# A recurrent time-mix on one core: score products on 32x32 tiles, added up in PSUM

## Chip, core and metric

The kernel runs on one core of one Trainium2 chip. The metric is the device time of one execution in microseconds. The time of the kernel before is the median of three runs.

## The reference, cut to what matters

Two parts are computed from the same normed rows and added to the input: a recurrent time-mix (16 heads of 32 channels, 2 sequences of 4096 tokens) and a layer of eight experts. The change is in the time-mix. Its recurrence is

```python
def step(S, inp):
    r_, w_, k_, v_, kk_, b_ = inp
    sab = jnp.einsum('bhvk,bhk->bhv', S, kk_)
    S = S * jnp.exp(w_)[:, :, None, :] + sab[..., None] * b_[:, :, None, :] + v_[..., None] * k_[:, :, None, :]
    y = jnp.einsum('bhvk,bhk->bhv', S, r_)
    return (S, y)
_, y = jax.lax.scan(step, S0, (rh, wh, kh, vh, kkh, bh))
```

The kernel doesn't step through tokens. It takes 32 tokens at a time as a chunk and, for each head, forms the products of queries (`kk` for the u part, `r` for the y part) with keys (`b` and `k`) of the same chunk, with the decay between them. Only earlier keys count: key < query for u, key <= query for y. The products are the entries of small triangular systems, which are inverted by doubling.

## The kernel before

**Tiles and stages.** The time-mix goes in 64 tiles of 128 columns, 64 tokens of each of the two sequences. Channels are on the partitions: 4 groups (G) of 128 channels, each with 4 heads (HG) of 32. A *unit* is one group, one sequence and one chunk of 32 tokens; a tile has U = 16 units. The work is a pipeline of five stages: N (norm the rows), A (projections), B (scores), C (inverse and state), D (output). One *turn* runs all five, each on another tile (`step`). 68 turns are laid out, most of them inside a loop whose body has 28 turns written out; scores are made in 64.

**Order.** Nothing schedules the work: each engine has its order written by hand (`DVE_STEPS`, `ACT_STEPS`, `POOL_STEPS`, `PE_STEPS`), and the functions `on_vector`, `on_scalar`, `on_gpsimd` and `on_tensor` issue it. Each step raises the engine's semaphore by one; others wait for the count. PSUM has eight banks, and `BANK` lists their tenants in order: `clear(e, name)` makes TensorE wait until the tenant before has been read.

**The scores (stage B).** Decay within a chunk is split in four *blocks* of eight queries (BLOCKS = 4): block j takes its reference at its own middle and needs keys 0 to 8j+7, so 8, 16, 24 and 32 keys, KEYS = 80 in all. VectorE makes the keys for the four blocks (`key_span`, `make_keys`) in `keys`: for each unit 2 x 80 columns (b and k). GpSimd makes the queries (`queries_of`, L774): for each of the four heads a product over 32 partitions, written into the head's own 32 columns of a 128-column slab, the rest of which is zero from a fill at the start. So a slab has the four heads' queries on its block diagonal, and TensorE (`score`, L877) needs one product for a unit: 128x128 weights, 160 columns moving. In the result each partition has a head's query and the columns are all four blocks' keys. For three units at a time (two in the last groups, `UNITS`) VectorE takes out what counts (`mask_scores`, L378): four predicated copies, one for each block, with a mask `known` of the queries of that block and the keys before them, into `raw`, which was filled with zero at the start. That is 6 groups x 4 blocks x 2 (u, y) = 48 predicated copies a turn. Their tenants in PSUM are u0 to u5 and y0 to y5, in banks 4 and 5 in turn, with `bonus` before u0 in bank 4, `out` in bank 4 and `gate` in bank 5.

**What stands around.** On TensorE the score groups stand between the products of the inverse (`P_of` L853, `Q_of` L864: 64 products on 32x32 tiles each, in two halves), the projections (`project` L829, 128x128), the low-rank ones (`low` L838), the output (`out_of` L947) and the state (`from_values` L891, `from_state` L905, `u_of` L915, `from_solved` L924: 32 products on 32x32 tiles each). In the 32x32 products head h uses partitions 32h to 32h+31 for its operands and its result. VectorE has `B.bonus` (L477), `D.acc` (L551, adds the stored rows to the output), the predicated copies of the inverse (`invert`, L403) and 32x32 transposes.

A float32 product shows as two matmul records in the trace, each with its own weight load.

Of the kernel before, what the change touches and what calls it, by code (L numbers as in the profile page):

```python
# [8 lines left out]
P = 128  # L9
# [80 lines left out]
UNITS = [(0, 3), (3, 6), (6, 9), (9, 12), (12, 14), (14, 16)]  # L90
# [26 lines left out]
def time_mix(nc, core, dram):  # L117
# [3 lines left out]
    with ExitStack() as ctx:  # L121
# [11 lines left out]
        for name, width in (("known", 4 * KEYS), ("levels", 5 * N)):  # L133
            wt[name] = sb(name, width, I32)
# [73 lines left out]
        known = wt["known"][:, :].rearrange("p (q o s k) -> p q o s k", q=2, o=1, s=2)  # L208
# [6 lines left out]
        heads_of = lambda q: queries[q][:, :].rearrange("p (n h j s) -> p n h j s", n=U, h=HG, j=BLOCKS)  # L215
# [25 lines left out]
        for g in range(G):  # L241
# [14 lines left out]
            "B.y5.3 A.scan A.b A.k2 C.rows1 C.shrunk1 C.state1").split()  # L256
# [5 lines left out]
            "B.rk B.eye B.qu0 B.qu1 B.qu2 B.qu3 B.qy0 B.qy1 B.qy2 B.qy3 C.faded0 A.lt B.us C.faded1 B.ys").split()  # L262
        PE_STEPS = (
            "A.x D.centre C.P0 A.mix A.scored C.Q0 D.var A.delta D.gate B.value C.P1 B.bonus A.gate1 A.low_wa A.delta3 B.u0 C.Q1 "
            "B.u1 A.low_k C.P2 B.u2 C.Q2 A.key B.u3 A.decay C.P3 B.u4 B.u5 A.low2 C.Q3 B.y0 B.y1 A.sums C.z0 B.y2 "
            "B.y3 C.u0 C.y0 D.out B.y5 B.y4 C.z1 C.u1 A.recept C.y1").split()
# [6 lines left out]
            ("centre", 4, dve, "D.normed"), ("bonus", 4, dve, "B.bonus"), ("u0", 4, dve, "B.u0.3"), ("u2", 4, dve, "B.u2.3"),  # L273
            ("u4", 4, dve, "B.u4.3"), ("y0", 4, dve, "B.y0.3"), ("y2", 4, dve, "B.y2.3"), ("out", 4, dve, "D.acc"),
            ("y4", 4, dve, "B.y4.3"), ("var", 5, act, "D.lnv"), ("gate", 5, dve, "D.gated"), ("u1", 5, dve, "B.u1.3"),
            ("u3", 5, dve, "B.u3.3"), ("u5", 5, dve, "B.u5.3"), ("y1", 5, dve, "B.y1.3"), ("y3", 5, dve, "B.y3.3"),
            ("y5", 5, dve, "B.y5.3"), ("P0", 6, act, "C.P0"), ("P1", 6, act, "C.P1"), ("P2", 6, act, "C.P2"),
# [63 lines left out]
        def on_vector(e, turn, on, out, got):  # L341
# [4 lines left out]
            def query_span():  # L346
                if "B.shrink" in act.was:
                    e.wait_ge(act.old, act.ago("B.shrink"))
                    e.wait_ge(pool.old, pool.ago(f"B.qy{HG - 1}"))
                e.tensor_tensor(by_block(dq), refs, spans, ALU.subtract).then_inc(dve.sem, dve.step("B.dq"))  # L350

            def key_span(j):
                if j == 3 and "B.y5" in pe.was:
                    e.wait_ge(pe.old, pe.ago("B.y5"))
# [12 lines left out]
            def mask_scores(q, m):  # L367
# [124 lines left out]
            if Bs:  # L492
                mask_scores("u", 0)
                mask_scores("u", 1)
            if A:
                lerp_of(3)
            if Bs:
                mask_scores("u", 2)
            if Cs:
                invert(2)  # L500
            if Bs:
                mask_scores("u", 3)
# [11 lines left out]
            if Bs:  # L514
                mask_scores("u", 4)
                mask_scores("u", 5)
                e.wait_ge(dve.sem, dve["B.u5.3"])
# [12 lines left out]
            if Bs:  # L530
                mask_scores("y", 0)
                mask_scores("y", 1)
# [5 lines left out]
            if Bs:  # L538
                mask_scores("y", 2)
# [7 lines left out]
                mask_scores("y", 3)  # L547
# [12 lines left out]
            if Bs:  # L560
                mask_scores("y", 4)
# [14 lines left out]
            if Bs:  # L576
                mask_scores("y", 5)
# [184 lines left out]
        def on_gpsimd(e, turn, on, out, got):  # L762
# [58 lines left out]
        def on_tensor(e, turn, on, out, got):  # L821
# [201 lines left out]
            if Bs:  # L1023
                score("u", 0)
# [687 lines left out]
```

## Time and profile before

| | |
|---|---|
| median of three runs | 6587.33 us (6576.18 to 6587.72) |
| the profiled execution, span | 6580.5 us |
| instructions in the profile | 269852 |
| TensorE matmul, busy | 5958.9 us (91%), 123464 |
| TensorE weight load, busy | 4298.1 us (65%) |
| VectorE, busy | 4111.1 us (62%), 9325 |
| ScalarE, busy | 1874.8 us (28%) |
| GpSimd, busy | 1465.7 us (22%), 1284 |
| mean granted TensorE clock | 0.955 |

How to read the profile: PE is TensorE's matmul side, PEld its weight loads, DVE VectorE, ACT ScalarE, POOL GpSimd, SP SyncE. Times are microseconds from the start of the span. A group of instructions is told by its line, engine and operation, with the tiles that it writes and reads, its shape and its count. An idle time has behind "<-" what ended it; "issue" means that nothing the profile shows did. The ends of matmuls are modelled and overlap the next start, so in a timeline the distance between starts is the safer measure.

### The profile page before, as it was taken

What the parts mean: (1) busy time and instruction counts of PE and PEld (TensorE: products, weight loads), DVE (VectorE), ACT (ScalarE), POOL (GpSimd) and SP (SyncE); (2) the same over time, 40 slices, a digit from 0 to 9 for tenths busy, and PEclk for the clock granted to TensorE, in tenths of its full rate; (3) what the DMA queues carried; (4) which work ended last, traced back from release to release, by engine and by line L of the source; (5) the groups of instructions that cost most, each with busy time, mean ns of one, the idle gap of its engine ahead of it and who ended that gap; (6) DMA issues with size and microseconds to landing.
All of it is one profiled execution on the core that took longest, in us unless ns stands there. A gap on an engine that the chain in (4) does not pass through costs nothing. (4 is left out here: it accounts for less than half of the span.)

```text
span 6580.5 us, 269852 instructions
## 1 busy us (share of the span) xinstructions
PE 5958.9 (91%) x123464; PEld 4298.1 (65%) x123464; DVE 4111.1 (62%) x9325; ACT 1874.8 (28%) x3531; POOL 1465.7 (22%) x1284
## 2 busy tenths in 40 slices
PE   6898898999998898998989898897499999999999
PEld 5777777777777777777777777776244444444443
DVE  6778787778777778777778778776424223322300
ACT  3333333333333333333333333332010000000010
POOL 1222222222222222222222222221202202221210
PEclk9999999999999999999999999998699999999999
DMA  1000000000000000000000000000211211121120
GB/s 56 20 18 17 20 19 16 18 21 16 20 20 16 19 21 16 18 21 16 18 21 16 17 23 16 17 21 10 92 45 57 81 58 66 59 91 45 66 71 13
DMA packets 108741, 212.80 MB, mean 32 GB/s; under 512 B 25424, under 2 KB 26704, under 8 KB 107088
## 3 DMA queue, kind: packets, MB, share of 16 engines
q1 hardware_dynamic: 92240, 144.98, 7.6%
q0 software_dynamic: 15360, 50.48, 2.3%
q8 instruction: 977, 16.01, 1.0%
q14 instruction: 164, 1.34, 0.1%
HBM read 144.67 MB, written 50.72 MB: 30 GB/s over the span
## 5 line engine op out<-in xcount | busy, mean ns | idle before, releaser
L378 DVE COPY_PREDICATED time_raw<-time_known,w_bank 128x96 f32<-128x96 int32 (+6 forms) x3072 | 823.4, 274 | 209.3 <-PE w_bank L877 127.9
L1664 PE MATMUL moe_bank<-moe_w,moe_hidden 128*128 128x512 f32 x2048 | 928.7, 596 | 0.0
L1651 PE MATMUL moe_bank<-moe_hT,moe_w 128*128 128x512 f32 x2048 | 923.3, 594 | 0.8 <-DVE moe_hT L1551 0.8
L1651 PEld LDWEIGHTS moe_bank<-moe_hT,moe_w 128*128 128x128 f32 x2048 | 386.4, 190 | 471.3 <-issue 470.1
L1664 PEld LDWEIGHTS moe_bank<-moe_w,moe_hidden 128*128 128x128 f32 x2048 | 379.4, 190 | 429.5 <-issue 428.1
L1572 ACT ACTIVATE moe_hidden<-moe_bank,moe_b 128x512 f32<-128x512 f32 x256 | 175.9, 687 | 1628.2 <-PE moe_bank L1651 1491.5
L806 POOL TENSOR_TENSOR time_tail<-time_tail,time_lp 128x512 f32<-128x512 f32 x64 | 75.4, 1178 | 2288.7 <-ACT time_lp L733 2222.2
L877 PE MATMUL w_bank<-time_keys,time_queries_u 128*128 128x160 f32 x2048 | 424.4, 353 | 146.9 <-DVE time_bonus L477 141.9
L864 PE MATMUL w_bank<-time_invT,time_part 32*32 32x32 f32 x32768 | 426.1, 201 | 123.7 <-issue 67.6
L864 PEld LDWEIGHTS w_bank<-time_invT,time_part 32*32 32x32 f32 x32768 | 363.3, 112 | 209.4 <-issue 143.3
L853 PEld LDWEIGHTS w_bank<-time_inv,time_ub 32*32 32x32 f32 x32768 | 348.0, 109 | 166.7 <-issue 129.4
L877 PEld LDWEIGHTS w_bank<-time_keys,time_queries_u 128*128 128x128 f32 x2048 | 347.5, 223 | 161.5 <-DVE time_bonus L477 148.7
L853 PE MATMUL w_bank<-time_inv,time_ub 32*32 32x32 f32 x32768 | 410.0, 198 | 45.5 <-issue 30.3
L774 POOL TENSOR_TENSOR time_queries_u<-time_dq,time_kkn 32x512 f32<-32x512 f32 x256 | 312.6, 1221 | 475.3 <-ACT time_dq L648 460.3
L403 DVE COPY_PREDICATED time_invT<-time_levels,w_bank 128x512 f32<-128x512 int32 x256 | 187.2, 731 | 362.4 <-PE w_bank L864 362.3
L1551 DVE COPY moe_hT<-moe_bank 128x512 f32<-128x512 f32 x64 | 44.2, 691 | 536.2 <-PE moe_bank L1638 536.2
L877 PE MATMUL w_bank<-time_keys,time_queries_y 128*128 128x160 f32 x2048 | 343.3, 310 | 27.5 <-DVE time_mixed L551 19.9
L774 POOL TENSOR_TENSOR time_queries_y<-time_dq,time_r 32x512 f32<-32x512 f32 x256 | 353.1, 1379 | 25.9 <-POOL time_queries_u L774 10.0
L877 PEld LDWEIGHTS w_bank<-time_keys,time_queries_y 128*128 128x128 f32 x2048 | 292.3, 191 | 82.8 <-DVE time_mixed L551 34.9
L393 DVE SCALAR_TENSOR_TENSOR time_lerp<-w_bank,time_maa,time_xx 128x128 f32<-128x128 f32 x1024 | 284.5, 340 | 55.5 <-PE w_bank L932 55.4
L829 PE MATMUL w_bank<-time_xf,time_value 128*128 128x128 f32 x2048 | 291.1, 293 | 0.1
L829 PE MATMUL w_bank<-time_xf,time_key_w 128*128 128x128 f32 x2048 | 283.1, 287 | 0.0
(227 smaller groups left out, 10059.2 us busy)
## 6 DMA issues: line engine op xcount, KB each, us to landing
moe_w<-in_w SPq DMA_DIRECT2D x64, 1024.0 KB, 7.4
mid_xn<-time_xn_rows SPq DMA_DIRECT2D x128, 129.0 KB, 2.5
time_x_rows<-in_x SPq DMA_DIRECT2D x128, 128.0 KB, 2.9
time_base<-in_x SPq DMA_DIRECT2D x128, 128.0 KB, 3.2
mid_acc<-time_mixed SPq DMA_DIRECT2D x128, 128.0 KB, 2.7
mid_scores<-time_rated SPq DMA_DIRECT2D x128, 2.0 KB
moe_b<-in_b SPq DMA_DIRECT2D x8, 256.0 KB
time_receptance<-in_w_receptance SPq DMA_DIRECT2D x1, 1024.0 KB, 5.0
```

The costliest lines, as they stand in the source:

```text
L378: e.copy_predicated(by_raw[:, "uy".index(q), n0:n1, :, 0:8 * j + 8], known[:, "uy".index(q), :, :, mine].to_broadcast([P, n1 - n0, 2, 8 * ...
L393: e.scalar_tensor_tensor(grp(lerp, g), grp(BANK[f"delta{f}"], g), wt["maa"][:, f * G + g:f * G + g + 1], grp(xx, g), ALU.add, ALU.mult).th ...
L403: e.copy_predicated(chunks(got["invT"]), level(lev + 1, U), chunks(BANK[f"Q{lev}"])).then_inc(dve.sem, dve.step(f"C.T{lev}"))
L774: e.tensor_tensor(heads_of(q)[head(h), :, h], by_block(dq)[head(h), :, :, at:at + 8], eights(by)[head(h)], ALU.mult).then_inc(pool.sem, po ...
L806: e.tensor_tensor(chunks(tail), chunks(tail), padded(lp)[:, :, 1:33], ALU.add).then_inc(pool.sem, pool.step("A.lt"))
L829: mm = e.matmul(ps[:, o * P:(o + 1) * P], weight[:, g * width + o * P:g * width + (o + 1) * P], rhs_of(g), start=g == 0 and (o == 0 or not ...
L853: mm = e.matmul(BANK[f"P{lev}"][head(h), blk(n)], got["ub"][head(h), blk(n)], got["inv"][head(h), blk(n)], start=True, stop=True, skip_gro ...
L864: mm = e.matmul(BANK[f"Q{lev}"][head(h), blk(n)], part[head(h), blk(n)], got["invT"][head(h), blk(n)], start=True, stop=True, skip_group_c ...
L877: mm = e.matmul(BANK[f"{q}{m}"][:, (n - n0) * 2 * KEYS:(n - n0 + 1) * 2 * KEYS], queries[q][:, n * P:(n + 1) * P], keys[:, n * 2 * KEYS:(n ...
L1572: e.activation(hidden[now % 4][:, :], up[now % 3][:, :], ACT.Gelu_apprx_tanh, bias=b1[:, x * FC + k:x * FC + k + 1]).then_inc(act.sem, act ...
L1651: got = e.matmul(up[now % 3][:, :], w1[:, g * F + k * P:g * F + (k + 1) * P], hT[x % 2][:, g * CAP + half * HALF:g * CAP + (half + 1) * HA ...
L1664: got = e.matmul(down[t][:, :], hidden[now % 4][:, t * P:(t + 1) * P], tile(w2, k), start=k == 0, stop=k == FC - 1)
```

## The change

Scores are made for each head and block by itself. A query slab now has four blocks of 32 columns, one for each block of eight queries; block j has its eight queries in columns 8j to 8j+7 and zero elsewhere, for all four heads at once (each head on its own 32 partitions). GpSimd writes a slab in one instruction for u and one for y. TensorE takes, for each unit, blocks 3, 2, 1, 0 and in each the four heads: a product on a 32x32 tile with 2 x (8j+8) columns moving, added in PSUM to what is there; block 3 starts the sum and writes all 32 keys. As the other queries' columns are zero, each query's row ends with its own block's score. In PSUM a unit then has 2 x 32 columns, and eight units fill a bank. VectorE needs one predicated copy of 128x512 for eight units, with one causal mask that no longer knows blocks. The orders of steps and the tenants of banks follow: u0, y0 in bank 4, u1, y1 in bank 5, and TensorE issues the scores in six places, of four or eight units.

```diff
-UNITS = [(0, 3), (3, 6), (6, 9), (9, 12), (12, 14), (14, 16)]
+UNITS = [(0, 8), (8, 16)]
...
-        for name, width in (("known", 4 * KEYS), ("levels", 5 * N)):
+        for name, width in (("known", 2 * N), ("levels", 5 * N)):
...
-        heads_of = lambda q: queries[q][:, :].rearrange("p (n h j s) -> p n h j s", n=U, h=HG, j=BLOCKS)
+        eights_of = lambda q: bass.AP(tensor=queries[q], offset=0, ap=[[U * P, P], [P, U], [N + 8, BLOCKS], [1, 8]])
...
         PE_STEPS = (
-            "A.x D.centre C.P0 A.mix A.scored C.Q0 D.var A.delta D.gate B.value C.P1 B.bonus A.gate1 A.low_wa A.delta3 B.u0 C.Q1 "
-            "B.u1 A.low_k C.P2 B.u2 C.Q2 A.key B.u3 A.decay C.P3 B.u4 B.u5 A.low2 C.Q3 B.y0 B.y1 A.sums C.z0 B.y2 "
-            "B.y3 C.u0 C.y0 D.out B.y5 B.y4 C.z1 C.u1 A.recept C.y1").split()
+            "A.x D.centre C.P0 A.mix A.scored C.Q0 D.var A.delta D.gate B.value C.P1 B.bonus A.gate1 A.low_wa A.delta3 C.Q1 "
+            "B.u0 A.low_k C.P2 C.Q2 A.key A.decay C.P3 B.u1 A.low2 C.Q3 A.sums C.z0 B.y0 "
+            "C.u0 C.y0 D.out B.y1 C.z1 C.u1 A.recept C.y1").split()
...
                 e.wait_ge(pe.sem, pe[f"B.{q}{m}"])
-                got_ = BANK[f"{q}{m}"][:, 0:(n1 - n0) * 2 * KEYS].rearrange("p (n s k) -> p n s k", s=2, k=KEYS)
-                for j in range(BLOCKS):
-                    if j:
-                        e.wait_ge(dve.sem, dve[f"B.{q}{m}.{j - 1}"])
-                    mine = slice(key_at(j), key_at(j + 1))
-                    e.copy_predicated(
-                        by_raw[:, "uy".index(q), n0:n1, :, 0:8 * j + 8],
-                        known[:, "uy".index(q), :, :, mine].to_broadcast([P, n1 - n0, 2, 8 * j + 8]),
-                        got_[:, :, :, mine]).then_inc(dve.sem, dve.step(f"B.{q}{m}.{j}"))
+                e.copy_predicated(
+                    by_raw[:, "uy".index(q), n0:n1],
+                    known[:, "uy".index(q)].to_broadcast([P, n1 - n0, 2, N]),
+                    BANK[f"{q}{m}"][:, :].rearrange("p (n s t) -> p n s t", s=2, t=N)).then_inc(
+                    dve.sem, dve.step(f"B.{q}{m}"))
...
             def queries_of(q, at, by):
-                for h in range(HG):
-                    e.wait_ge(pool.sem, pool[f"B.q{q}{h}"] - 1)
-                    e.tensor_tensor(heads_of(q)[head(h), :, h], by_block(dq)[head(h), :, :, at:at + 8],
-                                    eights(by)[head(h)], ALU.mult).then_inc(pool.sem, pool.step(f"B.q{q}{h}"))
-                e.wait_ge(pool.sem, pool[f"B.q{q}{HG - 1}"])
+                e.tensor_tensor(eights_of(q), by_block(dq)[:, :, :, at:at + 8], eights(by), ALU.mult).then_inc(
+                    pool.sem, pool.step(f"B.q{q}"))
...
-            def score(q, *which):
-
-                for m in which:
+            def score(q, m, part_=(0, 8)):
+
+                if part_[0] == 0:
                     clear(e, f"{q}{m}")
                     e.wait_ge(dve.sem, dve["B.kk0"])
-                    e.wait_ge(pool.sem, pool[f"B.q{q}{HG - 1}"])
-                    n0, n1 = UNITS[m]
-                    for n in range(n0, n1):
-                        mm = e.matmul(BANK[f"{q}{m}"][:, (n - n0) * 2 * KEYS:(n - n0 + 1) * 2 * KEYS],
-                                      queries[q][:, n * P:(n + 1) * P], keys[:, n * 2 * KEYS:(n + 1) * 2 * KEYS],
-                                      start=True, stop=True, skip_group_check=True)
+                    e.wait_ge(pool.sem, pool[f"B.q{q}"])
+                n0, n1 = UNITS[m]
+                into = BANK[f"{q}{m}"][:, :].rearrange("p (n s t) -> p n s t", s=2, t=N)
+                for i in range(*part_):
+                    for j in reversed(range(BLOCKS)):
+                        for h in range(HG):
+                            mm = e.matmul(into[head(h), i, :, 0:8 * j + 8],
+                                          queries[q][head(h), (n0 + i) * P + j * N:(n0 + i) * P + (j + 1) * N],
+                                          by_key[head(h), n0 + i, :, key_at(j):key_at(j + 1)],
+                                          start=j == BLOCKS - 1, stop=j == 0, skip_group_check=True)
+                if part_[1] == n1 - n0:
                     mm.then_inc(pe.sem, pe.step(f"B.{q}{m}"))
...
-    mask = np.stack([(query // 8 == block) & m for m in (key < query, key <= query) for _ in "bk"], 1)
+    mask = np.stack([i < t, i <= t], 1)
```

In TensorE's order the scores move so: u0 (all eight units) stands behind both halves of the second Q (`Q_of(1, 1)`); the first half of u1 before `P_of(3, 0)`, its second half before `Q_of(3, 0)`; the first half of y0 before `from_values(0)`, its second half before `u_of(0)`; y1 before `from_values(1)`. On VectorE the mask of u0 follows `C.uk`, that of u1 follows `C.yk`, that of y0 follows `C.z0`, that of y1 follows `A.fk`.

## Rows read from the trace of the kernel before

**Rows 1.** The page: busy time, share of the span and instructions of each engine.

```profile
PE 5958.9 (91%) x123464; PEld 4298.1 (65%) x123464; DVE 4111.1 (62%) x9325; ACT 1874.8 (28%) x3531; POOL 1465.7 (22%) x1284
```

**Rows 2.** Windows: stretch, length, busy time (count) by engine, clock, DMA share, GB/s.

```profile
2028.60:2098.47 69.87, 63.95 (x1850) 53.76 (x1850) 55.30 (x131) 26.29 (x51) 17.22 (x15) 0.95 0.08 19
4400.00:4600.00 200.00, 164.25 (x5391) 134.65 (x5395) 131.12 (x307) 59.34 (x108) 37.17 (x34) 0.91 0.05 13
4600.00:4800.00 200.00, 103.56 (x1021) 58.71 (x1010) 90.67 (x179) 14.98 (x23) 39.02 (x33) 0.66 0.23 76
```

**Rows 3.** TensorE's waits: waiter, releaser, us in total, times, longest.

```profile
PE w_bank L877 <- DVE time_bonus L477: 141.9, 61, 3.9
PE w_bank L864 <- issue: 67.6, 60, 1.8
...
PE w_bank L877 <- DVE time_mixed L551: 19.9, 62, 0.7
```

**Rows 4.** The page's groups: busy us, mean ns of one, idle before.

```profile
L378 DVE COPY_PREDICATED time_raw<-time_known,w_bank 128x96 f32<-128x96 int32 (+6 forms) x3072 | 823.4, 274 | 209.3 <-PE w_bank L877 127.9
...
L806 POOL TENSOR_TENSOR time_tail<-time_tail,time_lp 128x512 f32<-128x512 f32 x64 | 75.4, 1178 | 2288.7 <-ACT time_lp L733 2222.2
...
L774 POOL TENSOR_TENSOR time_queries_u<-time_dq,time_kkn 32x512 f32<-32x512 f32 x256 | 312.6, 1221 | 475.3 <-ACT time_dq L648 460.3
L403 DVE COPY_PREDICATED time_invT<-time_levels,w_bank 128x512 f32<-128x512 int32 x256 | 187.2, 731 | 362.4 <-PE w_bank L864 362.3
...
L774 POOL TENSOR_TENSOR time_queries_y<-time_dq,time_r 32x512 f32<-32x512 f32 x256 | 353.1, 1379 | 25.9 <-POOL time_queries_u L774 10.0
```

**Rows 5.** Timeline of TensorE in a turn: start, us, group, count.

```profile
2080.87 1.90 PE L877 MATMUL w_bank<-time_keys,time_queries_y 128*128 128x160 f32 x12
2082.70 0.75 PE L915 MATMUL w_bank<-time_rhs,time_invT 32*32 32x32 f32 x64
2083.38 1.98 PE L947 MATMUL w_bank<-time_output,time_mixed 128*128 128x512 f32 x4
...
2091.43 1.16 PE L829 MATMUL w_bank<-time_xf,time_receptance 128*128 128x128 f32 x8
2092.52 1.10 PE L905 MATMUL w_bank<-time_by_state,time_state 32*32 32x64 f32 x64
2093.54 2.05 PE L829 MATMUL w_bank<-time_xf,time_receptance 128*128 128x128 f32 x16
2095.52 0.75 PE L915 MATMUL w_bank<-time_rhs,time_invT 32*32 32x32 f32 x64
```

**Rows 6.** The page's DMA queues: packets, MB, share of 16 engines.

```profile
q8 instruction: 977, 16.01, 1.0%
```

**Rows 7.** Timeline of TensorE near 4540 us; idle time before in brackets.

```profile
4539.95 1.08 PE L864 MATMUL w_bank<-time_invT,time_part 32*32 32x32 f32 x104 [0.66 <-issue]
4540.96 1.08 PE L877 MATMUL w_bank<-time_keys,time_queries_u 128*128 128x160 f32 x6
4542.70 0.33 PE L853 MATMUL w_bank<-time_inv,time_ub 32*32 32x32 f32 x17 [0.66 <-DVE time_raw L378]
4543.67 1.14 PE L853 MATMUL w_bank<-time_inv,time_ub 32*32 32x32 f32 x111 [0.65 <-issue]
4544.74 1.35 PE L877 MATMUL w_bank<-time_keys,time_queries_u 128*128 128x160 f32 x8
4546.02 0.26 PE L864 MATMUL w_bank<-time_invT,time_part 32*32 32x32 f32 x8
4547.52 1.22 PE L864 MATMUL w_bank<-time_invT,time_part 32*32 32x32 f32 x120 [1.23 <-issue]
4548.67 1.22 PE L877 MATMUL w_bank<-time_keys,time_queries_y 128*128 128x160 f32 x7
4551.47 0.95 PE L877 MATMUL w_bank<-time_keys,time_queries_y 128*128 128x160 f32 x5 [1.59 <-issue]
...
4555.59 0.31 PE L905 MATMUL w_bank<-time_by_state,time_state 32*32 32x64 f32 x7 [0.90 <-issue]
```

More of the change, by code:

```diff
@@ L250, in time_mix @@
             "B.kb1 B.kk1 B.kb0 B.kk0 B.bonus D.bonus D.gated C.T1 C.I1 "
[5 rows of a table removed]
-            "B.y5.3 A.scan A.b A.k2 C.rows1 C.shrunk1 C.state1").split()
[2 rows of a table added]
+            "B.ub C.T3 B.pairs B.inv "
+            "A.min C.z0 B.y0 B.vT B.kT B.bT "
+            "D.acc C.rows0 C.shrunk0 C.state0 A.kkn C.z1 A.wmk A.g1 A.p2 A.fk B.y1 "
+            "A.scan A.b A.k2 C.rows1 C.shrunk1 C.state1").split()
         ACT_STEPS = (
@@ L272, in time_mix @@
             ("rated", 3, dve, "A.rated"), ("delta0", 3, dve, "A.lerp03"), ("gate1", 3, act, "A.hid_g"), ("key", 3, dve, "A.kkn"),
[L273 to L277, printed above, removed]
+            ("centre", 4, dve, "D.normed"), ("bonus", 4, dve, "B.bonus"), ("u0", 4, dve, "B.u0"), ("y0", 4, dve, "B.y0"), ("out", 4, dve, "D.acc"),
+            ("var", 5, act, "D.lnv"), ("gate", 5, dve, "D.gated"), ("u1", 5, dve, "B.u1"),
+            ("y1", 5, dve, "B.y1"), ("P0", 6, act, "C.P0"), ("P1", 6, act, "C.P1"), ("P2", 6, act, "C.P2"),
             ("P3", 6, act, "C.P3"), ("sums0", 6, act, "C.y0"), ("sums1", 6, act, "C.y1"), ("Q0", 7, dve, "C.T0"), ("Q1", 7, dve, "C.T1"),
@@ L348, in query_span @@
                     e.wait_ge(act.old, act.ago("B.shrink"))
-                    e.wait_ge(pool.old, pool.ago(f"B.qy{HG - 1}"))
+                    e.wait_ge(pool.old, pool.ago("B.qy"))
                 e.tensor_tensor(by_block(dq), refs, spans, ALU.subtract).then_inc(dve.sem, dve.step("B.dq"))
             def key_span(j):
-                if j == 3 and "B.y5" in pe.was:
-                    e.wait_ge(pe.old, pe.ago("B.y5"))
+                if j == 3 and "B.y1" in pe.was:
+                    e.wait_ge(pe.old, pe.ago("B.y1"))
                 e.tensor_tensor(key_units(1, j), padded(csum)[:, :, 1:8 * j + 9],
@@ L514, in on_vector @@
             if Bs:
-                mask_scores("u", 4)
-                mask_scores("u", 5)
-                e.wait_ge(dve.sem, dve["B.u5.3"])
+                mask_scores("u", 1)
+                e.wait_ge(dve.sem, dve["B.u1"])
                 if c_was:
@@ L790, in on_gpsimd @@
                 e.wait_ge(dve.old, dve.ago("A.kkn"))
-                if "B.y5" in pe.was:
-                    e.wait_ge(pe.old, pe.ago("B.y5"))
+                if "B.y1" in pe.was:
+                    e.wait_ge(pe.old, pe.ago("B.y1"))
                 queries_of("u", 0, kkn)
@@ L795, in on_gpsimd @@
                 e.wait_ge(act.old, act.ago("A.r"))
-                if "B.y5" in pe.was:
-                    e.wait_ge(pe.old, pe.ago("B.y5"))
+                if "B.y1" in pe.was:
+                    e.wait_ge(pe.old, pe.ago("B.y1"))
                 queries_of("y", 1, r)
@@ L1027, in on_tensor @@
             if Bs:
-                score("u", 1)
+                score("u", 0, (0, 4))
+                score("u", 0, (4, 8))
             if Cs:
@@ L1037, in on_tensor @@
                 key_of(0, 2)
-            if Bs:
-                score("u", 2)
             if Cs:
@@ L1048, in on_tensor @@
             if Bs:
-                score("u", 3)
+                score("u", 1, (0, 4))
             if Cs:
@@ L1061, in on_tensor @@
             if Bs:
-                score("u", 4)
-                score("u", 5)
+                score("u", 1, (4, 8))
             if Cs:
@@ L1077, in on_tensor @@
             if Bs:
-                score("y", 0)
-                score("y", 1)
+                score("y", 0, (0, 4))
             if Cs:
@@ L1089, in on_tensor @@
             if Bs:
-                score("y", 2)
-                score("y", 3)
+                score("y", 0, (4, 8))
             if Cs:
@@ L1102, in on_tensor @@
             if Bs:
-                score("y", 5)
-                score("y", 4)
+                score("y", 1)
             if Cs:
@@ L1179, in time_mix_inputs @@
     one = lambda name: d[name].reshape(1, C)
-    query, block = np.arange(P)[:, None] % N, np.repeat(np.arange(4), 8 * np.arange(1, 5))[None]
-    key = np.concatenate([np.arange(8 * j + 8) for j in range(4)])[None]
-    mask = np.stack([(query // 8 == block) & m for m in (key < query, key <= query) for _ in "bk"], 1)
+    mask = np.stack([i < t, i <= t], 1)
     heads = row // N == np.arange(P)[None] // N
```

21 lines of the change are left out of this document (4 added, 17 removed), and 7 rows, old and new, of the table DVE_STEPS.

## Prediction

> **How I read it.** The page comes first: TensorE's matmuls fill 91% of the span and VectorE 62% [rows 1]. That share is a mean over two stages, so the stretches come next. The change sits in the first of them, the time-mix; the expert matmuls behind it don't change. One turn of the time-mix, from one set of transposes of the normed rows to the next, takes 69.87 us (2028.60 to 2098.47), with 1850 matmul records, 63.95 us of them busy, at a mean granted clock of 0.95 [rows 2]. So in a turn TensorE has six idle microseconds and everybody else many more: it is the engine that sets the turn. There are 64 turns with scores (3072 masks at 48 a turn [rows 4]).
>
> The waits say what the six microseconds are: 141.9 us in all, 2.2 a turn, are the first score product waiting for VectorE's bonus (its bank is the bonus's), 19.9 us (0.3 a turn) are the product of y4 waiting for `D.acc`, and 67.6 us of one tiled line alone are put down to "issue", that is, to nothing that the profile shows [rows 3]. This last kind decides the case, so I followed it in the timeline.
>
> **What "issue" is.** Near 4540 us the turns run with less beside the tiled work, and the stall returns again and again: matmuls start anew, after an idle time that nothing releases, at 4539.95, 4543.67, 4547.52 and 4551.47 [rows 7]. Twice it cuts a group of tiled products in the middle, where no wait stands in the code. Count the records between: 104+6+17 = 127, then 111+8+8 = 127, then 120+7 = 127. Each matmul record has a weight load beside it, so 127 are 254 instructions, and a couple of semaphore waits make 256. The page lists a DMA queue of kind "instruction" with 977 packets and 16.01 MB [rows 6], 16.4 KB each; 2 x 123,464 TensorE instructions [rows 1] over 977 are 253 to a packet. So TensorE's program comes in pieces of 256 instructions, and where a piece is used up before the next is there, TensorE stands still. The spacings of those starts, 3.72, 3.85 and 3.95 us (mean 3.84), are what a piece costs when it is run through quicker than that. Only the first of the three has a wait for VectorE in it, and it is the shortest, so such waits don't make the spacing. I take the mean, and 3.72 for the low end. Today a turn has 2 x 1850 instructions, about 14.5 pieces in 69.9 us, or 4.8 us each: mostly slower than the fetch, so it shows in few places.
>
> The Trainium skill, in "Runtime: NRT & Kernel Launch", section "Instruction fetch mechanics", gives the same piece (16 KiB, 256 instructions) and says that the crossing is mostly hidden, since the sequencer fetches the next one meanwhile. The rows agree on the piece and not on the hiding: that rule would take the sum below to that of the first rival.
>
> **Part by part, for one turn.**
>
> *TensorE, removed:* 32 products of 128x128 weights with 160 columns, two records each, 64 records. Twelve of them take 1.83 us from their start to the next line's (2080.87 to 2082.70), 0.152 us each [rows 5]: 9.8 us.
>
> *TensorE, added:* 16 units x 4 blocks x 4 heads x 2 (u and y) = 512 products on 32x32 tiles; each is again two records, as in the 32x32 lines of today: 1024 records of 64, 48, 32 and 16 columns, a quarter each. Price by the array: 64 records of 32 columns take 0.68 us (2082.70 to 2083.38) [rows 5], 104 take 1.01 us (4539.95 to 4540.96) [rows 7]; the 40 more cost 0.33 us, so 8.25 ns each and 0.15 us for the change of shape. 64 records of 64 columns take 1.02 us (2092.52 to 2093.54) [rows 5], 13.6 ns each. For 16 columns I have no row; they are no dearer than 32 and, since the pitch is then no longer that of the columns, probably no cheaper: 8.25. 48 lies between: 11. The mean is 10.3 ns, 10.5 us a turn (8.4 if all went at 8.25). Accumulating instead of overwriting costs nothing in the 64-column row, which accumulates too.
>
> *Changes of shape:* eight full records take 1.09 us, sixteen 1.98 [rows 5], so 0.111 each and 0.20 fixed; with the tile's 0.15 a round trip between the shapes costs 0.35. The scores now stand next to tiled groups, and five full stretches disappear (between Q1 halves, before P2, before Q3, before `from_values(0)`, before `u_of(0)`): -1.7 us. By the array alone TensorE's turn gets 1.0 us shorter.
>
> *TensorE's program:* 960 more records, 1920 more instructions: 2 x 2810 = 5620 a turn, 22 pieces where it was 14.5. The added 2048 are 8 pieces, and each is run through in 128 x 10.3 ns = 1.3 us, so it costs the fetch's 3.84: 30.7 us. This is the step on which the sum hangs.
>
> *VectorE:* 48 masks a turn (823.4 us in all, 12.9 a turn) become four of 128x512 from PSUM; the predicated copy of that shape takes 731 ns [rows 4]: 2.9. Ten microseconds less, none on TensorE's path except through the bonus wait. That wait (2.2 us) goes: VectorE reaches `B.bonus` earlier, as GpSimd is beside it for a shorter time, and TensorE later; where it goes nothing else is late, for the fetch is then what ends last. The 0.3 us on `D.acc` goes as y1 is in bank 5.
>
> *GpSimd:* 8 products of 32x512 (1221 and 1379 ns, 10.4 us a turn) become two of 128x512, 1178 ns each by the nearest row [rows 4]; strided, up to 1.4. Eight microseconds less, hidden both before and after behind TensorE. Fewer semaphore steps: nothing.
>
> *Added waits:* u and y have two banks, not six tenancies. `out_of` needs the mask of y0, which starts when y0's last product is through and takes 0.73 us; `u_of(0)`'s 0.68 us stands between, so TensorE waits 0.1 to 0.3 us: +0.2. Behind it are only TensorE's own products. y1 in front of `from_values(1)` holds up the state by its length, which is already in the sum. Mask u1 has both halves of Q3 and the low-rank products to hide under. The smaller mask constant shortens one load at the start: nothing.
>
> *Clock:* the mean granted clock is 0.95 where TensorE is 92% busy (2028.60), 0.91 at 82% (4400), 0.66 at 52% (4600) [rows 2]. The new turn has some 62 us of work in 90, 70%: between the last two, 0.8. What would be slowed is the other work, some 50 us: at most 50 x (0.95/0.8 - 1) = 9 us. Most of that falls into pieces that wait for the fetch anyway or where the clock is up again, so I take 3, with 0 and 9 as ends.
>
> **The sum.** The rest of a turn: 69.9 - 9.8 (scores) - 2.2 - 0.3 (waits) - 1.7 (shape) + 0.2 = 56.1 us. With 30.7 for the eight pieces and 3 for the clock: 89.8 us, 19.9 more than 69.9. Times 64: +1274 us. Against the profiled execution (span 6580.5, 7 us under the median of the runs shown, which is 6587.3) this is 7855, against the median 7861. I predict 7860.
>
> Two errors in it work against each other: score groups don't begin at a piece's edge, so a piece that is half score and half slower work pays less than I count; and tiled P and Q groups next to them, now hidden half the time, fall under the fetch more often. Lower end: all 22 pieces of a turn at the shortest spacing, 3.72: 81.8 us, +11.9 x 64 = 762, 7350. Upper end: eight pieces at 4.12 us (the next spacing in rows 7, 4551.47 to 4555.59) and the clock's 9 us: 56.1 + 33.0 + 9 = 98.1, +28.2 x 64 = 1805, 8390. I round this to 8380.
>
> **Rivals.**
> 1. *The fetch is hidden* (faster). If a piece could be had as fast as it is run through, or several lay ready ahead, a turn would be 56.1 + 10.5 = 66.6 us, with the clock as now: -3.3 x 64 = -211, 6376. For it: most pieces cross without a stall today. Against: the four starts in a row at equal numbers of instructions, with 3.7 to 3.95 us between; had three or more pieces lain ready, the second and third stall could not be. The point at which it decides: the change loses time as soon as a dense piece costs over (69.9 - 56.1)/8 = 1.7 us. Chance 0.07. This is where the skill's "mostly hidden" would lead.
> 2. *The fetch comes later and the clock falls for good* (slower still). After a stall the next piece may come later (the one behind 4551.47 takes 4.12 us, again with nothing released in it), and a half clock after each of the six score groups slows what follows. 98 us a turn or above, 8390. For it: 0.66 at 52% busy. Against: the clock in a turn comes back quickly today. Chance 0.15, half of it above my range.
> 3. *The tiles don't overlap in accumulation* and go one after another: 4 x 10.3 = 41 ns a record, 42 us a turn in place of 30.7: 56.1 + 42 + 3 = 101, 8590. Against: the 64-column row. Chance 0.03.
> 4. *Pieces shared well*: pieces that are part score and part slow work balance each other, and a piece that is run through in 1.3 us, quicker than any in rows 7, has its successor asked for sooner than 3.72: a turn of 75 to 81 us, 6900 to 7350. For it: no row is as dense. Against it: nothing in the spacings falls with the work in them. Chance 0.08.
>
> The forecast has 0.66, and 0.01 is left for an end between rivals 1 and 4. So faster by over 0.2% (13 us, about what a measurement of this kernel can tell from no change) 0.07, within it 0.01, slower 0.92. The range leaves out rivals 1, 3 and 4 and half of rival 2, near 2 in 10 with a little over; I don't stretch it to 6900, since rival 4 has no row of its own behind it.
>
> **What would show it.** 184,904 TensorE matmuls; the instruction queue at some 24 MB; "issue" as TensorE's longest wait, over 1000 us in all, standing in the score line and at equal distances of 127 or 128 records, with 3.7 to 4 us between; TensorE's busy share in a turn near 70%; a turn of 85 to 95 us; VectorE's masks at 256 of about 0.73 us; no wait of the scores for the bonus. Right about the array: a score group without a stall in it has 10 ns a record. I'm wrong if 256-instruction pieces in the score line follow at under 3 us, or if the longest wait there is one for VectorE or GpSimd.

## The result, and the profile after

| | before | after |
|---|---|---|
| median | 6587.5 us (6576.2 to 6597.2, 4 runs) | 7863.7 us (7845.7 to 7876.1, 4 runs) |
| ratio to before | | 1.1936, 95% interval 1.1915 to 1.1957 |
| profiled execution, span | 6580.5 us | 7843.9 us |
| mean granted TensorE clock | 0.955 | 0.879 |

The change makes the kernel 19% slower, 1276 us, or 19.9 us for each of the 64 turns with scores. 7860 was forecast.

The page of after, busy time by engine, the clock in 40 slices, and the instruction queue (packets, MB, share of 16 engines):

```profile
PE 6531.3 (83%) x184904; PEld 4828.6 (62%) x184904; DVE 3280.0 (42%) x6509; ACT 1878.4 (24%) x3531; POOL 938.2 (12%) x900
...
PEclk8888888888888888888888888888877999999999
...
q8 instruction: 1456, 23.86, 1.3%
```

Against [rows 1] and [rows 6]: VectorE has 831 us less to do and GpSimd 528; both only stand idle longer. TensorE has 61,440 matmul records more, 960 in each of 64 turns, and its program is 7.85 MB longer.

One turn of after in the windows view, with the columns of [rows 2]:

```profile
2013.70:2104.50 90.80, 72.59 (x2817) 62.32 (x2818) 43.35 (x88) 26.32 (x51) 9.03 (x9) 0.85 0.06 16
```

The turn went from 69.87 to 90.80 us. Of the 20.9 us more, 8.6 are work (72.59 against 63.95, some of it the same work at the lower clock) and 12.3 are idle time.

TensorE's waits in after (waiter, releaser, us in total, times, longest); L859 is the score line, L832, L843, L875 and L899 are lines of tiled products that the change doesn't touch:

```profile
PE w_bank L859 <- issue: 597.1, 380, 3.0
PE w_bank L832 <- issue: 163.3, 115, 2.5
PE w_bank L843 <- issue: 94.6, 82, 2.4
PE w_bank L875 <- issue: 91.8, 65, 3.0
PE w_bank L899 <- issue: 65.9, 32, 2.7
...
PE w_bank L931 <- DVE time_raw L371: 9.3, 30, 0.3
```

These five are 1012.7 us, where [rows 3] began with 141.9 us of waiting for the bonus and 67.6 of issue. Over all lines of this view, issue is 1052.8 us, and 115.3 in the kernel before. So of the 1263 us by which the two profiled executions differ, 937 are more issue. The waits for other engines have become shorter together, and none of the five longest has a releaser. The last row is the wait that the change adds, the output product for the mask of y0, 0.15 us a turn.

What such a wait looks like, in the timeline of TensorE in that turn (start, us, group, count, idle before):

```profile
2035.36 0.84 PE L859 MATMUL w_bank<-time_keys,time_queries_u 32*32 32x64 f32 x64
2038.40 1.83 PE L859 MATMUL w_bank<-time_keys,time_queries_u 32*32 32x64 f32 x128 [2.19 <-issue]
2042.42 1.37 PE L859 MATMUL w_bank<-time_keys,time_queries_u 32*32 32x64 f32 x64 [2.19 <-issue]
2043.61 1.05 PE L832 MATMUL w_bank<-time_inv,time_ub 32*32 32x32 f32 x63
2046.29 0.21 PE L832 MATMUL w_bank<-time_inv,time_ub 32*32 32x32 f32 x1 [1.63 <-issue]
...
2055.02 1.50 PE L859 MATMUL w_bank<-time_keys,time_queries_u 32*32 32x64 f32 x128
2056.34 0.38 PE L832 MATMUL w_bank<-time_inv,time_ub 32*32 32x32 f32 x21
```

Count the records from one stall to the next: 128, then 64+63 = 127. That is [rows 7] again, now in the middle of the scores, with 4.02 and 3.87 us between. The group at 2055.02 has no stall inside: its 128 records take 1.32 us to the next group's start, 10.3 ns each. So a piece of the program that the array runs through in 1.3 us costs the turn close to four.

The counts say that the stalls keep step with the program; that it is the arrival of the program which ends them, the DMA view shows. From 2034 to 2044 us, in 40 slices of 0.25 us, nothing moves but three packets of the instruction queue, 16 KB each:

```profile
DMA  0000003000000000000000300000000000000030
GB/s 0 0 0 0 0 0 66 0 0 0 0 0 0 0 0 0 0 0 0 0 0 0 66 0 0 0 0 0 0 0 0 0 0 0 0 0 0 0 66 0
```

They start in the slices at 2035.5, 2039.5 and 2043.5 us, and TensorE goes on at 2038.40, 2042.42 and 2046.29, 2.8 to 2.9 us behind the slice's start each time. The whole trace has the same order. It holds 723 idle times of TensorE that are put down to issue; 98% of them end 1.2 to 1.6 us after a packet of this queue has ended. For matmul records picked at even distances that holds in 10% of cases. In the kernel before it is 95% of 137, against 7%. The medians in after make up the distance between stalls: from TensorE's new start to the next packet 1.2 us, the packet 1.1 us, from its end to TensorE's next start 1.4 us, 3.7 together. None of the three is work on the array.

VectorE's masks and GpSimd's queries in after (busy us, mean ns of one, idle before):

```profile
L371 DVE COPY_PREDICATED time_raw<-time_known,w_bank 128x512 f32<-128x512 int32 x256 | 185.4, 724 | 821.5 <-PE w_bank L859 821.5
L754 POOL TENSOR_TENSOR time_queries_y<-time_dq,time_r 128x512 f32<-128x512 f32 x64 | 76.9, 1201 | 0.0
```

### The profile page after: what moved, and what is told of

Read it like the earlier page. It is cut to its first block and busy times, and to the rows that moved or that the text cites. A ratio compares the mean times of both kernels' runs of the same rounds, so it can differ in the third digit from the quotient of the medians.

```text
span 7843.9 us, 388891 instructions
## 1 busy us (share of the span) xinstructions
PE 6531.3 (83%) x184904; PEld 4828.6 (62%) x184904; DVE 3280.0 (42%) x6509; ACT 1878.4 (24%) x3531; POOL 938.2 (12%) x900
## 3 DMA queue, kind: packets, MB, share of 16 engines
q8 instruction: 1456, 23.86, 1.3%
## 5 line engine op out<-in xcount | busy, mean ns | idle before, releaser
L859 PE MATMUL w_bank<-time_keys,time_queries_u 32*32 32x64 f32 (+3 forms) x32768 | 506.8, 216 | 343.7 <-issue 342.2
L859 PEld LDWEIGHTS w_bank<-time_keys,time_queries_u 32*32 32x32 f32 x32768 | 461.5, 122 | 381.4 <-issue 372.9
L859 PE MATMUL w_bank<-time_keys,time_queries_y 32*32 32x64 f32 (+3 forms) x32768 | 463.4, 207 | 257.0 <-issue 254.8
L859 PEld LDWEIGHTS w_bank<-time_keys,time_queries_y 32*32 32x32 f32 x32768 | 427.0, 114 | 328.6 <-issue 327.2
L832 PE MATMUL w_bank<-time_inv,time_ub 32*32 32x32 f32 x32768 | 467.5, 207 | 168.8 <-issue 163.3
L832 PEld LDWEIGHTS w_bank<-time_inv,time_ub 32*32 32x32 f32 x32768 | 397.2, 119 | 275.6 <-issue 245.5
L843 PE MATMUL w_bank<-time_invT,time_part 32*32 32x32 f32 x32768 | 440.5, 205 | 131.5 <-issue 94.6
L371 DVE COPY_PREDICATED time_raw<-time_known,w_bank 128x512 f32<-128x512 int32 x256 | 185.4, 724 | 821.5 <-PE w_bank L859 821.5
L843 PEld LDWEIGHTS w_bank<-time_invT,time_part 32*32 32x32 f32 x32768 | 380.4, 116 | 193.3 <-issue 157.6
L412 DVE STREAM_TRANSPOSE time_rhs<-w_bank 128x256 f32<-128x256 f32 x128 | 57.6, 450 | 934.8 <-PE w_bank L889 934.8
L875 PE MATMUL w_bank<-time_by_values,time_vT 32*32 32x96 f32 x8192 | 308.6, 309 | 94.8 <-issue 91.8
L875 PEld LDWEIGHTS w_bank<-time_by_values,time_vT 32*32 32x32 f32 x8192 | 259.7, 139 | 112.4 <-issue 109.4
L808 PE MATMUL w_bank<-time_xf,time_receptance 128*128 128x128 f32 x2048 | 308.9, 304 | 2.6 <-issue 2.6
```

What stands on the lines that cost most here:

```text
L371: e.copy_predicated(by_raw[:, "uy".index(q), n0:n1], known[:, "uy".index(q)].to_broadcast([P, n1 - n0, 2, N]), BANK[f"{q}{m}"][:, :].rearr ...
L412: e.transpose(chunks(rhs), sums[:, :, at["z"] // N]).then_inc(dve.sem, dve.step(f"C.z{c}"))
L808: mm = e.matmul(ps[:, o * P:(o + 1) * P], weight[:, g * width + o * P:g * width + (o + 1) * P], rhs_of(g), start=g == 0 and (o == 0 or not ...
L832: mm = e.matmul(BANK[f"P{lev}"][head(h), blk(n)], got["ub"][head(h), blk(n)], got["inv"][head(h), blk(n)], start=True, stop=True, skip_gro ...
L843: mm = e.matmul(BANK[f"Q{lev}"][head(h), blk(n)], part[head(h), blk(n)], got["invT"][head(h), blk(n)], start=True, stop=True, skip_group_c ...
L859: mm = e.matmul(into[head(h), i, :, 0:8 * j + 8], queries[q][head(h), (n0 + i) * P + j * N:(n0 + i) * P + (j + 1) * N], by_key[head(h), n0 ...
```

## The experiments

**The disputed cost by itself.** 2048 tiled records in a row ahead of the first turn of the kernel before:

```diff
         core.meet((core.consts_in, CONSTS))
+        for n in range(16 * 16):
+            for h in range(HG):
+                nc.tensor.matmul(psum[7][head(h), blk(n % 16)], wt["ident"][head(h), 0:N], wt["eye"][head(h), :],
+                                 start=True, stop=True, skip_group_check=True)
```

> The kernel before with 1024 products on 32x32 tiles of 32 columns (2048 records, 16 pieces) back to back ahead of the first turn, nothing beside them. Theory of the pieces: 16 x 3.6 us = 55 to 60 us longer, with a stall each 128 records. Rival (array): 2048 x 8.3 ns = 17 us longer, without stalls.

Measured: 6632.7 us in one execution, 44 us over the median of before on that chip (7 runs, 6578.8 to 6596.3). The products themselves take 58.7 us (28.00 to 86.67), within the 55 to 60. The first turn's transposes start at 86.67 us, where they start at 31.8 in before, so 3.8 us of the products fill time in which TensorE waited anyway; the other 11 us between 55 and 44 aren't explained, and a single execution can't settle them. Its timeline, TensorE:

```profile
28.00 2.99 PE L1139 MATMUL w_bank<-time_eye,time_ident 32*32 32x32 f32 x212 [1.03 <-PEq L80]
32.32 1.58 PE L1139 MATMUL w_bank<-time_eye,time_ident 32*32 32x32 f32 x128 [1.33 <-issue]
36.32 1.93 PE L1139 MATMUL w_bank<-time_eye,time_ident 32*32 32x32 f32 x128 [2.42 <-issue]
...
50.96 1.93 PE L1139 MATMUL w_bank<-time_eye,time_ident 32*32 32x32 f32 x128 [1.52 <-issue]
54.69 1.93 PE L1139 MATMUL w_bank<-time_eye,time_ident 32*32 32x32 f32 x128 [1.79 <-issue]
58.69 1.93 PE L1139 MATMUL w_bank<-time_eye,time_ident 32*32 32x32 f32 x128 [2.07 <-issue]
...
85.89 0.85 PE L1139 MATMUL w_bank<-time_eye,time_ident 32*32 32x32 f32 x44 [1.80 <-issue]
86.67 1.11 PE L956 MATMUL w_bank<-time_ident,time_xn_rows 128*128 128x128 f32 x4
```

No other engine works on these operands, no semaphore stands between the products, and TensorE still stops each 128 records, for 1.33 to 2.42 us. From 32.32 to 85.89 there are fourteen pieces: 53.57 us, 3.83 us each, at 3.45 to 4.01. Only at the start does more than one piece seem to lie ready (212 = 84 + 128 records without a stall). This is the price that the forecast had taken from three spacings, 3.84. The granted clock is 0.52 in this stretch, near the lower level of 1.2 GHz, and a piece takes the array 1.93 us there. At that pace all 2048 records would be 31 us, so the low clock doesn't make the 58.7 either; and the pieces of [rows 7] came at the same distance while the tiled groups ran at full pace.

**The same number of products with more and with less work in each.** In the first all four blocks are replaced by block 3, and each product overwrites instead of adding; in the second every block has only its first eight keys, and the mask leaves out the rest:

```diff
-                    for j in reversed(range(BLOCKS)):
+                    for j in (3, 3, 3, 3):
...
-                                          start=j == BLOCKS - 1, stop=j == 0, skip_group_check=True)
+                                          start=True, stop=True, skip_group_check=True)
```

```diff
-                            mm = e.matmul(into[head(h), i, :, 0:8 * j + 8],
+                            mm = e.matmul(into[head(h), i, :, 0:8],
                                           queries[q][head(h), (n0 + i) * P + j * N:(n0 + i) * P + (j + 1) * N],
-                                          by_key[head(h), n0 + i, :, key_at(j):key_at(j + 1)],
+                                          by_key[head(h), n0 + i, :, key_at(j):key_at(j) + 8],
...
-    mask = np.stack([i < t, i <= t], 1)
+    mask = np.stack([(i < t) & (i < 8), (i <= t) & (i < 8)], 1)
```

> The change with the same count of products, but block 3's query columns and keys in all four places (the other blocks' scores are left out): every record has 64 columns instead of 16, 32, 48 and 64. Theory of the pieces: the array has room under the fetch (128 x 13.6 ns = 1.7 us of 3.6), so the time stays within 1% of 7864. Rival (array): (13.6 - 10.3) ns x 1024 x 64 = 216 us more, 8080.

> The change with the same count of products, but only the first eight keys for every block (the later keys are left out and masked): every record has 16 columns. Theory of the pieces: the same as after, 7800 to 7880, with 16 and 64 columns within 1.5% of each other. Rival (array): 1024 x 2.1 x 64 = 134 us less, 7730, and 350 us between 16 and 64 columns.

Measured: with 64 columns 7739.6 us (ratio to before 1.1759, 1.1732 to 1.1786), with 16 columns 7926.3 (1.2044, 1.2015 to 1.2072). Four times the work on the array is 187 us *faster*. That refutes the array as the bound, which wanted 350 us the other way. It is not what the pieces alone say either: they wanted 7785 to 7943 and 7800 to 7880, with the two within 1.5% of each other; the first is below, the second above, and the distance is 2.4%. The windows from 1000 to 4000 us of the kernels with 64 columns, of after, and with 16 columns, columns as in [rows 2]:

```profile
1000.00:4000.00 3000.00, 2415.43 (x94463) 2055.40 (x94462) 1438.07 (x2907) 885.27 (x1717) 304.32 (x305) 0.94 0.07 16
```

```profile
1000.00:4000.00 3000.00, 2401.97 (x92732) 2040.02 (x92731) 1406.29 (x2840) 870.40 (x1684) 297.60 (x297) 0.86 0.06 16
```

```profile
1000.00:4000.00 3000.00, 2411.45 (x91510) 2033.63 (x91505) 1392.19 (x2812) 862.56 (x1668) 297.53 (x297) 0.80 0.06 16
```

The granted clock is 0.94, 0.86 and 0.80 in this order. What it does to the products that the change doesn't touch can be read from the groups view: added up over all of the time-mix but the scores, their busy time is 3772, 4047 and 4229 us, and 3613 in before. The pieces don't differ: where a piece holds nothing but scores, it takes 3.53, 3.57 and 3.56 us. So the added work is free under the fetch, and with it the clock stays up for the slower products beside the scores. The clock is a second cost of its own in after, some 7863.7 - 7739.6 = 124 us, 1.9 us a turn. Probably it is more, for with 64 columns the untouched products still take 159 us longer than in before. (The two medians are from different chips; by the ratios to before it is 117. The kernel with 64 columns also overwrites where after adds up, which isn't tested apart.)

**Fewer products.** Only block 3, and only blocks 3 and 1:

```diff
-                    for j in reversed(range(BLOCKS)):
+                    for j in (BLOCKS - 1,):
...
-                                          start=j == BLOCKS - 1, stop=j == 0, skip_group_check=True)
+                                          start=True, stop=True, skip_group_check=True)
```

```diff
-                    for j in reversed(range(BLOCKS)):
+                    for j in (3, 1):
...
-                                          start=j == BLOCKS - 1, stop=j == 0, skip_group_check=True)
+                                          start=j == 3, stop=j == 1, skip_group_check=True)
```

> The change with only block 3 of the four scored for each unit and head (blocks 0 to 2 left out of the sum): 256 score records a turn in place of 1024, all with 64 columns. 768 records, 1536 instructions, 6 pieces fewer. Theory (pieces of 256 instructions, some 3.6 to 3.8 us each where they are run through quicker): a turn of 90 falls by 20 to 23 us, over 64 turns to 6400 to 6580 us. Rival (the array or its tiles set the price, at 8 to 11 ns a record): 768 x 9.5 ns = 7 us a turn less, 7400 us.

> The change with blocks 3 and 1 alone (the other two are left out): 512 score records a turn, 1024 instructions, 4 pieces fewer than after. Theory of the pieces: 14 to 15 us a turn less, 6900 to 6970 us, and the steps from 256 to 512 to 1024 records cost alike for each record, some 25 ns. Rival (array): 512 x 8.5 ns = 4.4 us a turn less, 7580.

Measured: 6452.7 us (ratio 0.9801, 0.9776 to 0.9826) and 6813.0 us (1.0350, 1.0324 to 1.0376). The first is within the pieces' range and 950 us from the rival's. The second is 87 us below my range. From 256 to 512 records a turn a record costs 360.3 us / (256 x 64) = 22 ns, from 512 to 1024 1050.7 / (512 x 64) = 32 ns, so "alike" was wrong. Issue over all lines is 271 us with one block, 627 with two, 1053 with four. That the first pieces still find slow work beside them to hide under and the later ones don't would fit this; it isn't shown apart. Both slopes are far above the 8 to 14 ns of the array. Note also that the change with a quarter of its products is 126 us, 2%, faster than before. Not all of it is the relief of VectorE and GpSimd, for its scores are also less work for TensorE: 256 records at 13.6 ns are 3.5 us a turn, where 9.8 were removed.

**The count alone, on the kernel before.** The old scores stay; behind each of the 12 groups come 40 tiled products into columns that nobody reads, 960 records a turn:

```diff
+                    for n in range(10):
+                        for h in range(HG):
+                            mm = e.matmul(BANK[f"{q}{m}"][head(h), 3 * 2 * KEYS:3 * 2 * KEYS + N], queries[q][head(h), blk(h)],
+                                          keys[head(h), 0:N], start=True, stop=True, skip_group_check=True)
```

> The kernel before with 40 more 32x32 products of 32 columns behind each of its 12 score groups, into PSUM columns that nobody reads: 960 records a turn more, just as many as the change adds. Nothing else is changed. Theory of the pieces: 22 pieces a turn as after, minus what is now between them, 7600 to 7950 us. Rival (array): 960 x 8.3 ns and 8 changes of shape, 11 us a turn, 7280.

Measured: 8009.7 us (ratio 1.2157, 1.2132 to 1.2181), 60 above my range and 730 above the rival. The kernel before becomes as slow as after by added records alone, and with hardly a change of the clock: it is 0.94 from 1000 to 4000 us, where before has 0.95. Issue over all lines is 732 us, 617 more than in before. With the rival's 11 us a turn for the work itself (704 us) that makes 1321 of the 1421 us. It has kept the wait for the bonus, 145.2 us, and its old scores, which after has not; that this is why it ends above after is likely, but not tested.

**The same products in other places.** Everything is computed, but the scores stand in sixteen places of two units instead of six of four or eight (two of the places as an example):

```diff
             if A:
                 clear(e, "key")
-                key_of(0, 2)
+                key_of(0, 1)
+            if Bs:
+                score("u", 0, (4, 6))
+            if A:
+                key_of(1, 2)
+            if Bs:
+                score("u", 0, (6, 8))
```

> The change with its scores in sixteen places of two units (64 records) between slower products, in place of six places of four or eight units; everything is computed. Theory of the pieces: hardly a piece is all scores any more, so most have 2 us and more of work under the fetch: 22 pieces at 3.6 to 3.8 us plus the slow ones' excess, 83 to 86 us a turn, 7450 to 7650 us, and a clock above 0.88. Rival (price per record, wherever it stands): no gain, and some 8 more changes of shape at 0.35 us, 8000 us.

Measured: 7672.1 us (ratio 1.1654, 1.1634 to 1.1674), 192 us faster than after and 22 above my range; the rival wanted 8000. Issue over all lines fell from 1053 to 777 us. The clock rose too, to 0.89 between 1000 and 4000 us, so the gain needn't be all the fetch's. By an estimate it can't come back to before: 22 pieces at the 3.6 us of after's score pieces are 79 us, over the 69.9 of a whole turn.

**What is worth having in it.** Two moves on the kernel before, old scores. The first puts both halves of the second Q ahead of u0 (`PE_STEPS` follows):

```diff
             if Cs:
                 Q_of(1, 0)
-            if Bs:
-                score("u", 0)
-            if Cs:
                 Q_of(1, 1)
             if Bs:
+                score("u", 0)
                 score("u", 1)
```

The second makes GpSimd wait with the y queries:

```diff
+                if A:
+                    e.wait_ge(dve.sem, dve["A.xf2"])
                 queries_of("y", 1, r)
```

> The kernel before with one move alone: both halves of the second Q in front of u0's product. Its 0.68 us goes into the bonus wait of 2.2 us, and one change of shape (0.35 us) goes: 1.0 us a turn, 6510 to 6530 us. Rival (the wait is what VectorE dictates, and work taken out in front of it only makes it longer behind): 6570 to 6600.

> The kernel before with the other move alone: GpSimd makes the y queries behind VectorE's A.xf2. If GpSimd beside VectorE is what makes VectorE late for the bonus (its products of 128x384 took 1.55 and 1.44 us there, against 0.68 for 128x512 elsewhere), the bonus wait falls from 2.2 us a turn to under 0.7, 6450 to 6500 us. Rival (the bonus is late for other reasons): 6580.

> The kernel before with two moves of order and its old scores: both halves of the second Q stand in front of u0's product, and GpSimd makes the y queries only when VectorE is through with A.xf2. The bonus wait (2.2 us a turn) and part of the wait for xf2 (0.8) go, and one change of shape (0.35): 2.5 to 3.4 us a turn, 6370 to 6430 us. Rival (the wait is passed on to the next piece of code or the next wait): 6560 to 6590.

Measured: the first alone 6515.2 us (0.9889, 0.9866 to 0.9912), within its range, the second alone 6399.1 (0.9717, 0.9697 to 0.9736), 51 below its range, both 6401.7 (0.9723, 0.9707 to 0.9739), within. The second alone and both together are the fastest kernels of this case, 2.8% under before, and can't be told from each other. The reason lies in VectorE's key products in front of the bonus, those of blocks 2 and 1. The two of block 2 in the groups view by shape, in before and then with the y queries later:

```profile
L361 DVE TENSOR_TENSOR time_keys<-time_keys,time_b 128x384 f32<-128x384 f32 x64 | 97.4, 1522 | 0.0
L364 DVE TENSOR_TENSOR time_keys<-time_keys,time_k 128x384 f32<-128x384 f32 x64 | 87.6, 1369 | 2.2
```

```profile
L361 DVE TENSOR_TENSOR time_keys<-time_keys,time_b 128x384 f32<-128x384 f32 x64 | 36.1, 565 | 0.0
L364 DVE TENSOR_TENSOR time_keys<-time_keys,time_k 128x384 f32<-128x384 f32 x64 | 36.6, 572 | 2.2
```

1522 and 1369 ns beside GpSimd, 565 and 572 without it; with the two of block 1 (1008 to 434 ns, 556 to 429) they are 157 us less, 2.5 us a turn. The price is small: `A.xf` stands beside GpSimd more often, 968 ns in place of 874. The Trainium skill ("SBUF — State Buffer", "SBUF: two separate sides") says that a GpSimd instruction and a VectorE one with two SBUF inputs take turns at a shared pair of ports, each for its whole length; this product has two SBUF inputs, and the rows agree. The wait for the bonus, 141.9 us in [rows 3], is 3.7 us. With it gone the first move has nothing left to fill, which is the likely reason why both together are no better than the second alone; alone it had taken 42 us off this wait (100.4 left), and the wait for `xf` takes 63.6 us with both, 61.9 without the first move. The 193 us that the second move gains are more than the 138 of the wait. The clock rose from 0.95 to 0.98; what the rest consists of wasn't taken apart.

**Tiled work in longer rows.** Both moves, and in five more places the halves of P and Q stand together. One of the five:

```diff
-            if A:
-                low("low_k", 2)
             if Cs:
                 P_of(2, 1)
+            if A:
+                low("low_k", 2)
```

> Both moves, and in five more places the halves of P and Q stand together, the slower product before or behind them: 5 changes of shape fewer (1.7 us a turn) and 0.5 to 1 us less of waits for the copied part. By the array alone 6230 to 6260 us. Theory of the pieces: 128 tiled records in a row are a whole piece run through in 1.1 us, so a part comes back as issue, 6300 to 6400; if the pieces bind more than the shapes, above 6402.

Measured: 6493.1 us (0.9856, 0.9836 to 0.9876), 91 us slower than both moves without it, and past my range on the side that I had named for "the pieces bind more than the shapes". Its waits:

```profile
PE w_bank L855 <- issue: 116.4, 89, 2.9
PE w_bank L866 <- issue: 85.8, 67, 2.6
...
PE w_bank L1070 <- issue: 29.9, 17, 2.7
```

Issue over all lines is 266 us where both moves have 118. That the halves of P and Q are kept apart by slower products in the kernel before pays, and this is what it pays for.

## Why the prediction was right, step by step

*The bound.* The step on which the sum hung, that a piece of scores costs the distance at which TensorE's program arrives and not what the array needs, holds. The piece by itself measured 3.83 us where 3.84 was taken. Inside after, of some 150 pieces that hold nothing but scores, over nine in ten ended in a stall, and the mean length was 3.6 us: those with a stall at either end take 3.8, those that begin without one 3.3. So the eight cost 28.8 us and not 30.7; this term was 1.9 us too large.

*The clock, and the neighbours.* Here the error went the other way. 0.85 was granted where I had worked out 0.8, but what is left of the turn is 90.8 - 28.8 = 62.0 us, against 56.1 + 3 = 59.1. So, if the other terms hold, clock and tiled groups that newly fall under the fetch are 5.9 us together, not 3. The sum had priced the clock and named the second as an error without a price. The traces show both. Issue on the four tiled lines that the change doesn't touch went from 99 to 416 us, 4.9 us a turn, part of which replaces waits for other engines. The clock accounts for the 1.8 to 1.9 us of the run with 64 columns and probably more. As an estimate: between those runs 0.41 to 0.45 of what the untouched products got longer showed in the time (187 of 457 us, 124 of 275), and against before they got 434 longer, so some 3 us a turn.

*The number.* The two errors nearly cancel: 89.8 us were forecast for a turn and this one has 90.80; the median turn went from 70.59 to 90.44. The hit to within 4 us of 7864 is luck. That the loss lies near 20 us a turn, with the eight pieces as its largest part, is not. The chances had a slip: what the range left out adds up to a quarter, where the text has two in ten with a little over.

*Busy share.* I had named 70% as a mark. It is 80% (72.59 of 90.80). I counted 62 us of work at the old clock; at the new one they would be 69 (62 x 0.95/0.85), and the rest of the difference isn't explained.

*The array.* 10.3 ns a record was worked out, and 10.3 is what the group without a stall shows. For products with 16 columns there is still no row without a stall, but the kernel made only of them isn't faster, so their price decides nothing here.

*VectorE and GpSimd.* 724 ns a mask (731 taken), 1201 ns for the y queries (1178 to 1400 taken), nothing of it on the path. VectorE's relief is 13 us a turn, not ten, since its key products no longer stand beside GpSimd: the 128x384 one takes 552 ns, 1522 in before. The wait for the bonus is gone (0.2 us in all), for the reason that was given, and the added wait of the output product is 0.15 us (0.1 to 0.3 taken).

*The marks.* 184,904 records, 23.86 MB (24), over 1000 us of issue, in the score line first, 127 or 128 records apart: all there, but for the busy share.

*The rivals.* That the fetch is hidden (0.07) is refuted by the dense stretch: by this rule of the Trainium skill, "Runtime: NRT & Kernel Launch", section "Instruction fetch mechanics", the crossing should mostly cost nothing, and there it costs 1.3 to 2.4 us each time. That tiles don't overlap while accumulating (0.03) falls with the 10.3 ns. The late fetch with a falling clock (0.15) was half right: the clock did fall, to no such price, and no piece of the dense stretch took over 4.01 us. Shared pieces (0.08) exist, and the spread kernel shows what sixteen places give, together with the clock that rose: 192 us.

## What to carry to other kernels

Count instructions as well as columns. Where a stretch of small products runs through 256 TensorE instructions (128 matmul records with their weight loads) in under some 3.6 us, the program's arrival is the bound: each further record costs 28 to 30 ns there (3.6 to 3.8 us over 128), with 16 columns in it as with 64. Here one larger product that does needless work beats sixteen exact ones. Idle time with releaser "issue" at equal counts of records, each ending some 1.4 us behind a packet of the instruction queue, is its mark in a profile; and before cutting a loaded engine's work, look whether a neighbour on the same ports merely makes it slow at the wrong moment.

## What the runs showed of the hardware that I had not expected

More work on the array made a kernel faster: from 16 to 64 columns in 1024 records a turn the clock rose from 0.80 to 0.94 and the time fell by 187 us. A single wait for GpSimd took a VectorE product from 1522 to 565 ns and the kernel from 6592 to 6399 us. And TensorE's instruction pieces of 16 KB, back to back, came 3.83 us apart, while one packet of their queue takes 1.1 us.
